# A hybrid Mamba, expert and attention kernel: convolution of two sequences on TensorE, layer norms in two ScalarE passes, first gate bank in another order

## The reference

```python
# 1, mixer: xn = rms-normed; hidden, gate = split(xn @ in_w + in_b)       # 2 x 256 channels
xp = pad(hidden, 3 in front)
h = silu(sum(conv_w[k] * xp[:, k:k+T] for k in range(4)) + conv_b)
ts, B, C = split(h @ xproj_w)                     # 64, 16, 16
delta = softplus(ts @ dt_w + dt_b); A = -exp(A_log)
state = exp(A * delta) * state + delta * B * h    # 16 states a channel, over 256 steps
y = (sum over states of state * C) + D * h
x += (y * silu(gate)) @ out_w + out_b
# 2 and 4, experts: 8 experts with 352 inner channels, the 2 best of a router
x += sum_e w_e * ((up_e(x) * silu(gate_e(x))) @ down_e)
# 3, attention: u, v, base = silu(x @ W_uv + b); squared relu scores; one output product
```

## Time and profile before

| what | value |
|---|---|
| time, median of 3 runs | 637.37 us (636.89 to 638.24) |
| the profiled execution | 636.95 us |
| its span, first to last instruction | 635.2 us |
| PE busy | 585.7 us, 92% |
| DVE busy | 504.4 us, 79% |
| ACT busy | 388.5 us, 61% |
| POOL busy | 399.6 us, 63% |
| granted TensorE clock, mean | 0.983 of full speed |

### The profile page before, as it was taken

How to read it: one execution, slowest core, us unless ns; L and a number is a source line. 1 busy time by engine, 2 the same in 40 slices (tenths; PEclk the granted TensorE clock), 3 DMA queues, 4 the chain that set the end, 5 groups by cost and what they waited for, 6 DMA issues and landing times.

```text
span 635.2 us, 13045 instructions
## 1 busy us (share of the span) xinstructions
PE 585.7 (92%) x4500; PEld 543.7 (86%) x4500; DVE 504.4 (79%) x1113; ACT 388.5 (61%) x826; POOL 399.6 (63%) x374
## 2 busy tenths in 40 slices
PE   7388899789998999999999999899999999999997
PEld 7134687489998999899999999899989999999997
DVE  5797778877898889988998899889988996345453
ACT  6987636657757775867577766676576641606140
POOL 1696574579685987769787978698767773001000
PEclk9789999979999999999999999999999999999999
DMA  7952103102030403021212203030303000000000
GB/s 275 275 177 91 52 30 136 66 28 121 5 142 9 147 4 146 2 88 69 81 68 86 72 10 138 18 138 4 146 10 146 1 14 9 13 2 13 1 22 10
DMA packets 18323, 45.44 MB, mean 72 GB/s; under 512 B 2831, under 2 KB 13648, under 8 KB 13906
## 3 DMA queue, kind: packets, MB, share of 16 engines
q1 hardware_dynamic: 18258, 44.61, 20.1%
HBM read 40.15 MB, written 1.31 MB: 65 GB/s over the span
## 4 chain that ended last, share of the span: by engine, by line
PE 74%; DVE 9%; POOL 9%; ACT 3%; issue 3%; DMA 0%; DVEq 0%; SPq 0%; ACTq 0%; POOLq 0%
PE ps L1265 23%; PE ps L1094 14%; PE ps L1095 13%; PE ps L1096 13%; POOL st L521 4%; DVE st L965 3%; PE ps L1314 2%; PE ps L1215 2%; DVE ps L951 1%; DVE X L1057 1%; POOL yacc L534 1%; PE ps L1174 1%; PE ps L1326 1%; PE ps L1305 1%; POOL up_lo L443 1%
## 5 line engine op out<-in xcount | busy, mean ns | idle before, releaser
L521 POOL TENSOR_TENSOR st<-st,rows_ring 128x512 f32<-128x512 f32 x128 | 165.4, 1295 | 48.4 <-DVE st L965 48.3
L1265 PE MATMUL ps<-down,inner_ring 128*128 128x128 f32 (+1 forms) x1408 | 171.5, 274 | 0.0
L1265 PEld LDWEIGHTS ps<-down,inner_ring 128*128 128x128 f32 (+1 forms) x1408 | 165.5, 191 | 1.7 <-issue 1.0
L760 ACT ACTIVATE sg<-ps 128x512 f32<-128x512 f32 x176 | 104.3, 596 | 98.1 <-PE ps L1096 96.3
L1043 DVE TENSOR_TENSOR inner_ring<-sg,ps 128x512 f32<-128x512 f32 x176 | 119.0, 679 | 50.6 <-PE ps L1096 25.0
L965 DVE TENSOR_TENSOR_SCAN st<-dA,ps 128x512 f32<-128x512 f32 x128 | 154.9, 1212 | 3.1 <-ACT dA L711 2.1
L534 POOL TENSOR_TENSOR yacc<-yacc,st 128x512 f32<-128x512 f32 x96 | 123.5, 1286 | 4.8
L1094 PE MATMUL ps<-xhi,gate_hi 128*128 128x256 f32 x352 | 102.0, 290 | 16.8 <-DVE xlo L1003 16.6
L711 ACT ACTIVATE dA<-delta,A 128x255 f32<-128x255 f32 x256 | 105.4, 494 | 4.1 <-POOL delta L513 4.0
L1094 PE MATMUL ps<-xhi,up_hi 128*128 128x256 f32 x352 | 104.3, 296 | 0.9 <-DVE inner_ring L1043 0.6
L1096 PE MATMUL ps<-xhi,gate_lo 128*128 128x256 f32 x352 | 100.0, 284 | 0.0
(11 more groups left out here) (146 smaller groups left out, 871.1 us busy)
## 6 DMA issues: line engine op xcount, KB each, us to landing
rows_ring<-bc SPq DMA_DIRECT2D x32, 1024.0 KB, 5.0
moved_rows<-inner_ring SPq DMA_DIRECT2D x96, 32.0 KB, 1.8
inner_ring<-gate_w SPq DMA_DIRECT2D x1, 1408.0 KB, 7.8
inner_ring<-up_w SPq DMA_DIRECT2D x1, 1408.0 KB, 10.1
down<-down_w SPq DMA_DIRECT2D x2, 512.0 KB, 10.7
out<-X SPq DMA_DIRECT2D x8, 128.0 KB, 1.8
X<-x SPq DMA_DIRECT2D x1, 768.0 KB, 7.0
down<-down_w SPq DMA_DIRECT2D x1, 384.0 KB, 10.6
```

The lines of the kernel that those rows point to most:

```text
L521: nc.gpsimd.tensor_tensor(st[:, i % NST], st[:, i % NST], row, ALU.mult).then_inc(s["m_p"], 1)
L760: nc.scalar.activation(sg[:, k % 2], two(bank_of(q, 2 * j)), ACT.Silu).then_inc(s["f_sg"], 1)
L1265: ins = nc.tensor.matmul(bank_of(q, 2 * NP + e)[:, c * H:(c + 1) * H], act_in, down[0:rows, e, n, :], start=n == 0, stop=n == NB - 1)
```

## The change

- The convolution of sequence 1 and the second half of the channels of sequence 0 are done on PE: `diag` (DVE) writes, for each tap, the identity times that tap's weights into the buffer `sg` (free in the fill), and `m_cv` (PE) adds four fp32 matmuls a half in the bank of the norm chain. `m_h` then takes the bank with the convolution's bias, one pass a half. POOL has no convolution of sequence 1.
- The rows of the first state of sequence 0 are sent in a transfer of their own, ahead of the other three of that block.
- Due times: the decays of sequence 0 are moved up, `m_ln` before `m_pad` of sequence 1, the up splits (and the loading of the down weights) later. For sequence 1, product and scan of the first state and dx are put ahead of `m_gate` of sequence 0; the gate activation of sequence 1 is put behind the first norm's `n_hi`. 22 dummy matmuls ahead of `m_xp` become 3. `lo_rw` and `split_uv` keep their due times.
- `n_nb` moves to ACT: it negates the mean, subtracts it in two passes, which wait for the statistics only, and `n_norm` then multiplies by the power in two more. `n_stats` gets two waits for the norm before.
- The first gate bank of each expert stage is cleared by one matmul of a row of zeros; then the four matmuls that read the high part of the rows follow behind `n_hi`, and the two that read the low part behind `n_lo`.

```diff
+NPC = 2
-         "scan": ..., "early": [19.0, -8.7, -6.8, 0.1], ...
+         "scan": ..., "early": [10.0, -8.7, -6.8, 0.1], ...
-WARM = {"m_turn": 8, "m_ph": 2, "m_xp": 22, "sum": 2, "out": 6}
+WARM = {"m_turn": 8, "m_ph": 2, "m_xp": 3, "sum": 2, "out": 6}
-"split_up0": 82.09, "split_up1": 84.33, ..., "load_down": 90
+"split_up0": 91.09, "split_up1": 93.33, ..., "load_down": 93, ..., "diag1": 65.9, "diag0": 74.1
-"m_ln": [35.4, 0.8, 4.5] ... "m_dx": [0.68, 3.0, 2.4] ... "m_g": [36.8, 3.1, 0]
+"m_ln": [34.35, 0.8, 4.5] ... "m_dx": [0.68, -3.0, 2.4] ... "m_g": [36.8, 5.1, 0]
+LEAD = {"dbx": -7.25, "scan": -8.95}      # for state 0 of sequence 1
...
+                if g == 0:
+                    first = 2 * T
+                    sp.dma_start(rows_ring[:, 0:first], bc[u, 0:first].partition_broadcast(P)).then_inc(s["d_rf"], 16)
...
             def m_h(u):
+                if u < NPC:
+                    if u == 0:
+                        act.wait_ge(s["m_conv0"], 1)
+                        nc.scalar.activation(h[:, 0], conv[:, 0], ACT.Silu)
+                    act.wait_ge(s["m_cv"], u + 1)
+                    for it in range(0 if u else 1, IT):
+                        ins = nc.scalar.activation(h[:, it], two(chainps)[:, it], ACT.Silu, bias=v(V_CB + it))
+                    ins.then_inc(s["m_h"], 1)
+                    return
...
-            def n_norm(arg):
+            def n_nb(arg):
-                act.wait_ge(s["n_nb"], l + 1)
+                act.wait_ge(s["n_var"], l + 1)
+                nc.scalar.activation(n_b[:], n_mv[:, :, 0], ACT.Copy, scale=-1.0).then_inc(s["n_neg"], 1)
+                act.wait_ge(s["n_neg"], l + 1)
                 for c in range(NC):
-                    ins = nc.scalar.activation(n_xn[:, c, :], X[:, u, c, :], ACT.Identity, bias=n_b[:, c, 0:1],
-                                               scale=n_r[:, c:c + 1])
+                    nc.scalar.activation(n_xn[:, c, :], X[:, u, c, :], ACT.Identity, bias=n_b[:, c:c + 1]).then_inc(s["n_xc"], 1)
+            def n_norm(arg):
+                act.wait_ge(s["n_rstd"], l + 1)
+                for c in range(NC):
+                    act.wait_ge(s["n_xc"], NC * l + c + 1)
+                    ins = nc.scalar.activation(n_xn[:, c, :], n_xn[:, c, :], ACT.Copy, scale=n_r[:, c:c + 1])
...
+            def diag(it):
+                def part(_):
+                    for k in range(KC):
+                        ins = nc.vector.tensor_tensor(taps[:, it, k], ident[:], v(V_CW + it * KC + k).broadcast_to([P, P]), ALU.mult)
...
+            def m_cv(u):
+                pe.wait_ge(s[f"w_diag{0 if u else 1}"], 1)
+                free("chain")
+                pe.wait_ge(s["m_pad"], u + 1)
+                for it in range(0 if u else 1, IT):
+                    for k in range(KC):
+                        ins = nc.tensor.matmul(two(chainps)[:, it], taps[:, it, k], xpad[:, it, k:k + T], start=k == 0, stop=k == KC - 1)
...
+                first = two(bank_of(q, 0))
+                nc.tensor.matmul(bank_of(q, 0), ones_rows[2 * LOW:2 * LOW + 1, :], rowb[2 * LOW:2 * LOW + 1, :], start=True, stop=False)
+                pe.wait_ge(s["n_hi"], norms["q", q] + 1)
+                for k in range(2):
+                    nc.tensor.matmul(first[:, k], gate_hi[:, cols[k]], xhi[q % 2][:], start=False, stop=False)
+                    nc.tensor.matmul(first[:, k], gate_lo[:, cols[k]], xhi[q % 2][:], start=False, stop=False)
+                pe.wait_ge(s["n_lo"], norms["q", q] + 1)
+                for k in range(2):
+                    ins = nc.tensor.matmul(first[:, k], gate_hi[:, cols[k]], xlo[q % 2][:], start=False, stop=k == 1)
```

More of the change, by code:

```diff
@@ L169, in build_plan @@
             plan.append((reached, "decay", (s, n)))
-            put(scan + step * n + PACE[("first", "second", "third", "later")[min(s, 3)]][n], STATE, (s, n))
+            put(scan + step * n + PACE[("first", "second", "third", "later")[min(s, 3)]][n],
+                {name: lag + (LEAD.get(name, 0) if (s, n) == (1, 0) else 0) for name, lag in STATE.items()}, (s, n))
         put(scan, {"m_dx": AT["dx"], "m_y0": AT["y0"]}, s)
@@ L298, in build @@
         in_raw = rows_ring[:, 0:2 * IT * P]
+        taps = sg[:].rearrange("p a b t -> p (a b t)").rearrange("p (a k c) -> p a k c", a=IT, k=KC)
         rowb_raw = at_s[0:LOW + 1].rearrange("p a t -> p (a t)")
@@ L626, in m_tap0 @@
             def m_tap0(u):
+                if 0 < u < NPC:
+                    return
                 act.wait_ge(s["m_pad"], u + 1)
@@ L630, in m_tap0 @@
                     act.wait_ge(s["m_h"], u)
-                for it in range(IT):
+                for it in range(IT if u else 1):
                     ins = nc.scalar.activation(conv[:, it], xpad[:, it, 0:T], ACT.Identity, bias=v(V_CB + it),
@@ L903, in m_conv @@
                 for k in range(1, KC):
-                    for it in range(IT):
+                    for it in range(1):
                         ins = nc.vector.scalar_tensor_tensor(out=conv[:, it], in0=xpad[:, it, k:k + T],
@@ L912, in m_conv @@
                 ins.then_inc(s["m_conv0"], 1)
+            def diag(it):
+                def part(_):
+                    dve.wait_ge(s["w_const"], 1)
+                    dve.wait_ge(s["d_vecs"], 16)
+                    for k in range(KC):
+                        ins = nc.vector.tensor_tensor(taps[:, it, k], ident[:], v(V_CW + it * KC + k).broadcast_to([P, P]), ALU.mult)
+                    ins.then_inc(s[f"w_diag{it}"], 1)
+                return part
             def m_v(u):
@@ L989, in n_stats @@
                     dve.wait_ge(s["a_x"], u + 1)
+                if norms[arg]:
+                    dve.wait_ge(s["n_neg"], norms[arg])
+                    dve.wait_ge(s["n_rstd"], norms[arg])
                 norm_stats(u, n_bn, n_mv)
                 nc.vector.tensor_scalar(n_ve[:], pairs(n_mv[:, :, 1:2]), EPS, None, ALU.add).then_inc(s["n_var"], 1)
-            def n_nb(arg):
-                l = norms[arg]
-                dve.wait_ge(s["n_rstd"], l + 1)
-                nc.vector.scalar_tensor_tensor(out=n_b[:], in0=pairs(n_mv[:, :, 0:1]), scalar=-1.0,
-                                               in1=pairs(n_r[:].unsqueeze(2)), op0=ALU.mult, op1=ALU.mult).then_inc(s["n_nb"], 1)
             def n_lo(arg):
@@ L1235, in gate @@
                     pe.wait_ge(sem, value)
-                if j == 0:
-                    pe.wait_ge(s["n_lo"], norms["q", q] + 1)
-                products(bank_of(q, 2 * j), (gate_hi, gate_lo), q, j).then_inc(s["f_G"], 1)
+                if j:
+                    products(bank_of(q, 2 * j), (gate_hi, gate_lo), q, j).then_inc(s["f_G"], 1)
+                    return
+                first = two(bank_of(q, 0))
+                cols = [slice((2 * NE + k) * P, (2 * NE + k + 1) * P) for k in range(2)]
+                nc.tensor.matmul(bank_of(q, 0), ones_rows[2 * LOW:2 * LOW + 1, :], rowb[2 * LOW:2 * LOW + 1, :], start=True, stop=False)
[6 more added lines that the diff above has]
+                    ins = nc.tensor.matmul(first[:, k], gate_hi[:, cols[k]], xlo[q % 2][:], start=False, stop=k == 1)
+                ins.then_inc(s["f_G"], 1)
             def up(arg):
```

79 lines of the change are left out of this document (44 added, 35 removed).

## The result

The changed kernel took 627.53 us (median of 4 runs, 624.79 to 628.66) against 637.79 us (4 runs) in the same set: ratio 0.9842, 95% interval 0.9818 to 0.9865. In a later set it took 626.20 (5 runs, 624.65 to 626.66) against 636.96; over its nine runs the median is 626.35. The forecast was 626.3. It is 10 to 11 us faster, and two of the forecast's terms were off in opposite directions.

The account below looks back on a forecast made before the run. Taken as bounds: how early the first sequence's scan is through, then PE's work and idling. Gains 2.2 + 2.1 + 0.9 + 5.5 = 10.7 off the profiled 636.95 gave 626.3 us; own range 624 to 629, stated range 623 to 632.

Parts of the forecast that it names:

- Fill, 2.2 us: Before the first expert stage: earlier scans, held at scan 4 by the router weights' split, gain 2.2 us.
- cover of 1.1 us: Start of the fill: taps and PE's products end near 11.4, 1.1 us ahead of ACT's gate splits.
- First stage, 2.1: First expert stage: shorter norm path and earlier high half bring DVE's first inner product 2.1 us forward.
- Second stage, 0.9: Second expert stage: norm path 0.4 us shorter, high half first gains more at PE's lower clock; 0.9 us together.
- rival 2: More gained: lo_rw unstalled, or PE's clock stays up in the second stage (2.8 us); 623.5, both 621; chance 0.18.
- The others, 13 x 0.42 = 5.5: Fourteen later expert stages, one counted as nothing: high half first saves 0.42 us each, 5.5 in all.
- the stage with the wait for POOL at 192: Expert stage at 169: PE later waits 0.45 us for POOL at 192.37, so no gain was counted.
- Rival 1: Expert stages: an earlier bank only moves PE's wait to the next one; without the 5.5, 631.8 us; chance 0.15.
- Rivals 3 and 4: 3: PE's low clock slows fill sums, 639 us, chance 0.08. 4: ACT's 26 us of further passes eat gains, 636.5, 0.07.

Follow-up runs that it names:

- after_again: The changed kernel unaltered, measured again in a later set: 626.20 us (5 runs).
- without_norm_with_dummies: The changed kernel with the old norm (bias product on DVE, one ACT round) and dummy matmuls ahead of PE's two convolutions: 628.92 us.
- late_router_split: The changed kernel with DVE's small split of the router weights behind scan 6 instead of ahead of scan 4: 624.38 us.

## Why the prediction was right, and where it wasn't

- **Fill, 2.2 us.** In the first profile the steps came as worked out (forecasts in brackets): conv 1.52, gate splits 9.96 to 12.58, the logarithm at 18.79, delta 0.69, scan 0 at 21.79 (21.6), lo_rw released by ACT's copy, scan 4 at 31.41 (31.8), the gate at 57.77 (57.7). Two deviations cancelled in it: scan 4 gained 2.6 instead of 2.2, and dx, with 2.51 instead of 0.70, took 0.5 of that back, since PE's last sum had ended at 57.25. And that is the second fastest of nine runs. By the rest of 567.1 their median has the gate at 59.2 (an estimate), 0.6 to 0.8 us of gain against the kernel before (59.88 in its profile, 60.0 by its median of 637.1 and its rest). What failed is the sentence on PE's four products beside DVE's taps, "some 1.9: two such matmuls with two loads each took 1.10". That price is for the full clock. They took 1.97 in one run and 3.75 in another, and that is beyond the cover of 1.1 us that the text gave. I had thought of PE's clock at 43 us, not at 8, where the change first puts PE on the way to h. The gate weights' arrival, on which the earlier splits depend, had no term either.
- **First stage, 2.1.** 2.05 to the high half. The first inner product, which the term was worked out for, came at 67.59, not 67: 1.8 us gained behind the gate multiplication, since y0 and a sum of sequence 1 stand on PE ahead of the clearing matmul (64.93). The two rounds of norm took 0.69 and 0.68 (0.7 taken). The estimate of 0.68 from "ScalarE: Activation LUTs" of the Trainium skill, section "What ACT_TABLE_LOAD costs", agrees.
- **Second stage, 0.9.** 1.06 measured. The granted clock stayed at 1.00, as rival 2 had it, but its 2.8 us are not in the time: PE now waits 1.0 for the next sequence's h in that stretch, where it had no such wait. In after_again the clock did fall there, to 0.50 from 127.1 to 130.5, and this stretch was only 0.2 us longer than in the first profile.
- **The others, 13 x 0.42 = 5.5.** 6.78 measured. Nothing at the stage with the wait for POOL at 192 (0.07), as said, 1.41 from stage 5 to 6, and 5.30 in the other twelve, 0.44 each. The mis-sized term is the attention's norm: I priced the new norm only where an expert stage begins, and the 63.9 us of ACT's waiting for n_b only as room.
- Rival 1 is out: PE's waits between 100 and 600 us sum to 9.4 instead of 23.0. Rivals 3 and 4 are out: PE's clock was back at full level at 42.4, sums 8 to 15 are spaced by 1.73 us in the mean (44.02 to 56.13; one of 2.38 waited for POOL), and ACT had the room. The low clock that the forecast saw from 24 to 37 before lasted from 22.9 to 36.6. The first row's own transfer is worth 0, as costed; so is the second convolution, within 1 us.

So the mechanisms were the ones forecast, but that the total is so near is partly luck: the gain of the rest was put 1.55 us too small, that of the fill some 1.4 to 1.6 too large for the median run. The forecast was also taken off the one profiled execution (636.95) and not off the median of 637.37, from which it would be 626.7.

## What to carry to other kernels

Split each run at an event between two regimes; here one timestamp explained nearly all of the difference between profiles of kernels with the same rest, and showed which experiments could be compared. A granted clock of 1.00 at the very start may only mean that the record hasn't begun: compare the spacing of equal matmuls. When work moves to an engine that was off the path, price it at the engine's slow pace too and look at what kept that engine busy before. Parts that shorten the same wait don't add up: do each alone and undo each.

## What was not expected of the hardware

- A DVE multiplication of 128x512 with both inputs in SBUF took 2.51 us (dx at 53.31) beside two POOL products that ran back to back from 52.76 to 55.26, and 0.70 where POOL was idle; a four-element one (n_b, at 62.25 in without_norm_with_dummies) took 1.21 beside a POOL product of 1.26. "SBUF — State Buffer" of the Trainium skill, section "SBUF: two separate sides", has the one of the two engines that comes second at a shared port pair block for the other's whole instruction; the traces agree: n_b ended at 63.46, with the POOL product (63.45). In late_router_split it went the other way: dx took 0.71 and POOL's pair 2.96 instead of 2.50.
- PE's first rise to full clock came at 4.9 to 5.8 us in ten of the fourteen profiles and at 9.6, 10.4, 10.6 and 14.4 in the others, in one kernel at 4.86 and at 14.44. Until then the trace has no entry of the clock, the views show 1.00, and PE is at half pace: in all fourteen the first dummies, from 1.5 us on, start 0.21 us apart, and 0.11 after the rise.
